# Another order of the filling work in the main loop of a two-layer graph kernel

## What is computed

```python
def _L0_gnn_ref(x, adj, W1, b1, W2, b2):
    F = x.shape[-1]
    mask = (adj > 0.0).astype(x.dtype)
    W1a, W1b = (W1[:F], W1[F:])
    xj_proj = x @ W1a
    diff = x[:, :, None, :] - x[:, None, :, :]
    h = jax.nn.relu(xj_proj[:, :, None, :] + diff @ W1b + b1)
    hm = jnp.einsum('bjkh,bjk->bjh', h, mask)
    deg = jnp.sum(mask, axis=-1)
    return hm @ W2 + deg[..., None] * b2

def _L1_gnn_ref(h, A, W1, b1, W2, b2, W_ih, b_ih, W_hh, b_hh):
    m = jax.nn.relu(jnp.einsum('bnh,hk->bnk', h, W1) + b1)
    m = jax.nn.relu(jnp.einsum('bnh,hk->bnk', m, W2) + b2)
    msg = jax.nn.relu(jnp.einsum('bij,bjh->bih', A, m))
    gi = jnp.einsum('bnh,gh->bng', msg, W_ih) + b_ih
    gh = jnp.einsum('bnh,gh->bng', h, W_hh) + b_hh
    ...
    return (1.0 - z) * n + z * h

x = _layernorm(x + _L0_gnn_ref(x, adj, ...), axis=-1)
x = _layernorm(x + _L1_gnn_ref(x, adj, ...), axis=-1)
```

## Time and profile before

| | us |
|---|---|
| median of 3 runs | 949.64 |
| lowest, highest | 948.91, 949.88 |
| the profiled execution's own time | 949.64 |
| its span, first to last instruction | 947.9 |
| PE busy | 856.4 (90%) |
| DVE busy | 841.1 (89%) |
| ACT busy | 563.1 (59%) |
| POOL busy | 309.3 (33%) |

### The profile page before, as it was taken

The page is one execution under the profiler, slowest core; times in us unless marked ns, Lnnn a source line. Parts: engine busy times, 40 slices in busy tenths (PEclk is TensorE's granted clock), DMA queues, the critical chain, the costliest instruction groups (busy, mean ns, idle before and its releaser), DMA issues.

```text
span 947.9 us, 24988 instructions
## 1 busy us (share of the span) xinstructions
PE 856.4 (90%) x10132; PEld 598.1 (63%) x10132; DVE 841.1 (89%) x1055; ACT 563.1 (59%) x1627; POOL 309.3 (33%) x300
## 2 busy tenths in 40 slices
PE   2678889999999999999999999999999999999983
PEld 1345556767666666767666666777666666667652
DVE  5479999999999999999999999999999999998742
ACT  3433435666676656667675757667675757656442
POOL 2111111242423424242423424242433424242451
PEclk9769999999999999999999999999999999999987
...
DMA packets 31426, 53.27 MB, mean 56 GB/s; under 512 B 8138, under 2 KB 16973, under 8 KB 31309
## 3 DMA queue, kind: packets, MB, share of 16 engines
...
...
## 4 chain that ended last, share of the span: by engine, by line
PE 64%; DVE 18%; issue 11%; SPq 2%; ACT 2%; DMA 0%; POOL 0%; POOLq 0%; DVEq 0%
PE PS L772 16%; PE PS L781 11%; DVE AC L1094 8%; DVE AC L1083 5%; PE PS L625 3%; PE PS L758 3%; PE PS L838 3%; PE PS L855 2%; PE PS L646 2%; PE PS L826 2%; PE PS L764 2%; PE PS L601 2%; PE PS L612 2%; PE PS L849 2%; PE PS L570 1%
## 5 line engine op out<-in xcount | busy, mean ns | idle before, releaser
L1094 DVE SCALAR_TENSOR_TENSOR AC<-PS,AC 128x1152 f32<-128x1152 f32 (+1 forms) x288 | 351.1, 1219 | 43.0 <-PE PS L772 41.3
L1083 DVE SCALAR_TENSOR_TENSOR AC<-PS,AC 128x1152 f32<-128x1152 f32 (+1 forms) x288 | 350.8, 1218 | 22.6 <-PE PS L781 22.5
L772 PE MATMUL PS<-DM,VA 128*128 128x192 fp8e5 (+1 forms) x1152 | 135.6, 241 | 17.1 <-DVE AC L1083 13.7
L772 PE MATMUL PS<-DM,VB 128*128 128x192 fp8e5 (+1 forms) x1152 | 136.1, 241 | 0.0
L781 PE MATMUL PS<-DM,VB 128*64 128x192 fp8e5 (+1 forms) x1152 | 95.8, 245 | 32.7 <-DVE AC L1094 31.5
L772 PEld LDWEIGHTS PS<-DM,VA 128*128 128x128 f16 x1152 | 89.0, 100 | 44.3 <-DVE AC L1083 28.6
L781 PEld LDWEIGHTS PS<-DM,VB 128*64 128x64 f16 x1152 | 46.7, 109 | 91.2 <-issue 53.3
L772 PEld LDWEIGHTS PS<-DM,VB 128*128 128x128 f16 x1152 | 75.9, 98 | 37.1 <-issue 0.9
L781 PE MATMUL PS<-DM,VA 128*64 128x192 fp8e5 (+1 forms) x1152 | 98.9, 252 | 0.0
L1530 POOL MEMSET AC<- 128x768 f32 x32 | 24.0, 749 | 221.0 <-DVE DM L1064 145.0
L1537 POOL TENSOR_TENSOR AC<-AC,NNB 128x512 f32<-128x512 f32 x64 | 66.0, 1051 | 62.1 <-DVE DM L1061 39.6
...
## 6 DMA issues: line engine op xcount, KB each, us to landing
CW<-WM SPq DMA_DIRECT2D x128, 160.0 KB, 2.8
...
```

What stands on the lines that cost most here:

```text
L772: last = e.matmul(PS[:, b + i % 2, 256 * (i // 2) + cols.start:256 * (i // 2) + cols.stop], lhs[:, GRAPH[i], 0:128], d[:, i, :], start=Fal ...
L1083: e.scalar_tensor_tensor(dst, tiles(PS[:, b:b + 3, :])[:, :, cols], 0.0, dst, ALU.max, ALU.add).then_inc(s["sx"], 1)
L1094: e.scalar_tensor_tensor(dst, tiles(PS[:, b:b + 3, :])[:, :, cols], 0.0, dst, ALU.max, ALU.add).then_inc(s["sy"], 1)
```

## The change

Only the table `ORDER` differs; every step is still there, at another place.

```diff
 ORDER = (
-    ("s2", "p3pde", "te", "ep", "", "t", "", "dprtp", "r", "t", "repee4", "", "d", "pe", "rpd", "e", "p", "wpr0e", "c1"),
-    ("sd2p", "pp3", "", "t", "d", "etpp", "", "l4tcpt", "n", "dp", "d", "np", "d", "d", "w0ddrp", "", "pd", "dp", "1e"),
+    ("psp23", "pd", "et", "te", "", "t", "r", "pedp", "r", "et", "erpe", "p", "ed4", "p", "re", "d", "p", "wpre0", "c1"),
+    ("s2pd", "3pp", "", "t", "d", "tpp", "", "4teptn", "", "cdp", "d", "pl", "d", "wnd", "dd0p", "", "epdr", "", "d1p"),
 )
```

## The result

The changed kernel takes 956.09 us (median; 955.09 to 957.85), the kernel before 949.27 beside it: a ratio of 1.0078, 95% interval 1.0063 to 1.0091. It is 6.8 us slower. The direction was predicted, the size was not: the forecast was +14.5 us. The profiled execution took 956.57, its span is 954.9.

A forecast was written before the change was run, and what follows sets the result against it. PE and DVE were taken as almost equally busy, the loop changing by the DVE's waits for the PE. Even first rounds 9.6, middle 1.4 and odd steps 3.5 gave 14.5 us on 949.64: 964.1 us, range 954.5 to 970.

The forecast's parts named there:

- a1 to b2: Even step: 1.69 us instead of 1.29, since the PE has no lead to hide `s_ov`; loss 0.40.
- b9 to b1: Boundary from odd to even step: 4.05 us instead of 3.82, `rank_t` being new between `seeds` and b1.
- b1 to a1: Even step: 1.47 us instead of 1.75; the `dgen` is gone, but the PE needs a round and `rank_ov`.
- b2 to a2: Even step: 1.74 us instead of 1.29, the PE needing a round and `out0_a`; loss 0.45.
- a2 to a3: Even step: 2.58 us instead of 2.58 + 0.16, since `out0_a` no longer stands here; gain 0.16.
- even step, first rounds: Sum from the DVE's b9 to a3: 11.53 us instead of 10.89, a loss of 0.64 in each of 15 even steps.
- even step, middle: Moved `dgen` and `yt`, `v` 0 directly behind b6: bounds 0 and 0.5 us, taken as 0.1 in 14 steps.
- odd step, from b8: With `mask` moved ahead of b9, b8 starts 0.27 us late and b9 0.25 late, in 14 odd steps.
- The margins of ACT and POOL: Even step: ACT 0.05 us ahead of `s_ov`, POOL done near 465.5 before a1 at 465.8; both counted as nothing.
- second rival: ACT late: `s_ov` waits 0.3 us for `rank_t`'s copy, or `v` 0 costs 0.5; 968.6 to 969.7 us, chance 0.14.
- third rival: POOL starts ahead of the third `dgen`, which waits about 1 us; b1 some 0.6 late, 973.1 us, chance 0.03.
- fifth rival: Odd step and middle cost nothing, first gaps overlap better: 0.4 us a pair, 955.6 us, chance 0.12.

The follow-up runs named there:

- e13: Kernel before with `ov` ahead of `seeds` in even steps instead of behind b1, nothing else moved: 948.51 us, ratio 0.9992.
- e14: Kernel before with the second `yt` and ACT's `y` of even steps moved from ahead of b6 to behind it: 949.14 us, ratio 0.9986.
- e2: The odd tuple of the change with the even tuple of the kernel before: 952.2 us, ratio 1.0027.
- e1: The even half alone: the even tuple of the change with the odd tuple of the kernel before: 955.26 us, ratio 1.0046.
- e3: Kernel before with only the third `dgen` of even steps moved ahead of b1: 949.45 us, ratio 0.9999.

## Why the prediction was off

Its mechanism stood: three PE pieces in consecutive gaps, where the DVE had to wait for each, and b8 without its cover. Two terms of the sum failed, the one from a1 to b2 and the one for the middle. By its own terms, from the DVE's b9, with the measured times of step 16 and the means of steps 6 to 28:

| term | predicted | measured |
|---|---|---|
| b9 to b1 | 4.05 | 4.02 |
| b1 to a1 | 1.47 | 1.49 |
| a1 to b2 | 1.69 | 1.53 |
| b2 to a2 | 1.74 | 1.74 |
| a2 to a3 | 2.58 | 2.54 |
| even step, first rounds | +0.64 | +0.43 |
| even step, middle | +0.1 | -0.14 |
| odd step, from b8 | +0.25 | +0.15 to 0.20 |

**The term a1 to b2 failed.** It took the 0.71 us from a1 to `s_ov` for the price of a round ahead of a product of full width. The same rows held the contradiction: b3 took 0.63 in front of such a product. 0.1 of the 0.71 was `s_ov` waiting for ACT to leave the bank of `ov`: 464.09 + 0.69 = 464.78, `s_ov` at 464.83. The change copies `ov` earlier and pays 0.61. e13 shows it alone. The other 0.06 between 1.69 and 1.53 is only shifted: the PE takes 1.59 (466.87 to 468.46), but the DVE's a1 started 0.06 late for POOL. With the other small differences (a2 to a3 2.54, a round of 1.27 rather than 1.29) the even step costs 0.43: 15 x 0.21 = 3.2 us less.

**The term of the middle failed, and in its sign.** Its bounds were 0 and 0.5, with no reason given why it could not be a gain, and the distance between the two engines' starts of b6 was not looked at. The `dgen` ahead of b6 stood in a wait of the DVE that no row lists; moved behind a6, where the PE has the lead, it costs 0.33. In the changed kernel a5 to b6 is 1.29 (479.34 to 480.63), before 1.79 (476.75 to 478.54), and the `dgen` takes 0.33 back from a6 to b7: -0.17, of which -0.14 is left at the end of the step. Against the +0.1 of the sum that is 14 x 0.24 = 3.4 us less. e14 shows the hidden wait alone.

**The odd step was right in place, a little high in size.** b8 waits 0.25 (0.27 forecast); 0.05 to 0.1 of it is not there behind b9, by e2's pair 0.17 for the whole half: 14 x 0.08 = 1.1 us less. Together these are 7.7 us of the 14.5, which leaves 6.8; the sum is as good as that by chance. b1 of step 6 is only 0.1 us late, though steps 2 and 4 have the new order already; b1 of step 32 is 5.7 us late, the last b9 5.2, and the span 6.9, so 1.7 us of the whole are from behind the last round.

**The margins of ACT and POOL were put at nothing, and neither was quite nothing.** Both were reckoned against wrong times: by the prediction's own sum a1 starts at 460.05 + 4.05 + 1.47 = 465.57, not 465.8, and `s_ov` at 465.57 - 0.82 + 0.71 = 465.46, not 465.65, so ACT, done at 465.6, would have been late.

In the change `s_ov` does wait for ACT's second copy of `rank_t` in each even step. That is the second rival's wait, but it costs 0.06 and not 0.3 us (b1 to b2 3.02, in the even half alone 2.96); only in step 30, where `s_ov` is 0.80 behind a1, is it 0.2.

a1 waits for POOL in each even step, 0.05 us longer than for the PE, 0.35 in step 14 (the one such wait in the list) and 0.24 in step 30. It costs next to nothing, since b2 waits for the PE anyway, but the term b1 to a1 came out right with its help: without it (e1) it is 1.43, not 1.49.

The third rival's wait, a `dgen` held by POOL, is not in the change, where POOL begins 0.2 us behind the last `dgen`. That POOL began right behind two `dgen` before was no sign of shared ports: the row's bracket names a semaphore of the `dgen`, ACT's first copy of `seeds` had ended 0.17 us earlier, and in e3 POOL starts just as far behind that copy while a third `dgen` runs.

**The points that held.** The waits forecast, 0.75, 0.2, 0.4, 0.45 ahead of b1, a1, b2, a2, read 0.81, none listed, 0.17, 0.38; the one ahead of a1 is there all the same. The range, which reached down to the fifth rival, held the time by that alone; that rival, the same loss but half, is what happened, though not by its reason for the odd step.
